# A decoder layer on one core: the first rstd moved to ScalarE, mask work moved into the attention loop, broadcast rows behind the weights, high weight parts on GpSimd, wider value matmuls

## The reference

```python
x = x + attention(layernorm(x), Wq, bq, Wk, bk, Wv, bv, Wo, bo)      # softmax(Q K^T / sqrt(16)), causal
n = layernorm(x)
x = x + softmax(where(mask, n @ ctx.T / 16, -1e30)) @ ctx            # zero where a batch has no valid token
n = layernorm(x)
logits = n @ router.T + rb;  score = softmax over the 4 largest logits
gate, up = (n @ gate_up[e] + bias)[..., ::2], [..., 1::2]            # all 16 experts e
x = x + sum_e score[e] * ((clip(up)+1) * min(gate,7) * sigmoid(1.702 gate) @ down[e] + dbias[e])
```

## Time and profile before

| | |
|---|---|
| time, median of 3 runs | 230.55 us (229.61 to 231.19) |
| profiled execution: its own time | 230.47 us |
| its span in the profile | 228.6 us |
| TensorE busy | 216.3 us, 95% |
| VectorE busy | 173.0 us, 76% |
| ScalarE busy | 127.8 us, 56% |
| GpSimd busy | 87.8 us, 38% |
| first matmul of the attention loop | us 16.54 |
| first matmul of the context scores | us 59.81 |

### The profile page before, as it was taken

How to read it: one execution, slowest core, us unless ns; L and a number is a source line. 1 busy time by engine, 2 the same in 40 slices (tenths; PEclk the granted TensorE clock), 3 DMA queues, 4 the chain that set the end, 5 groups by cost and what they waited for, 6 DMA issues and landing times.

```text
span 228.6 us, 4527 instructions
## 1 busy us (share of the span) xinstructions
PE 216.3 (95%) x1466; PEld 180.2 (79%) x1466; DVE 173.0 (76%) x434; ACT 127.8 (56%) x247; POOL 87.8 (38%) x67
## 2 busy tenths in 40 slices
PE   7899989998799799989999999999999999999995
PEld 2577857876478599768878988988988988998994
DVE  3489876779357755688798898898889789779655
ACT  2128999874343412835847657566476485395440
POOL 6622269941001100044254455447428428428000
PEclk9999999999799999999999999999999999999999
DMA  5993042000000000004214304404412322310002
GB/s 145 323 409 125 1 140 94 3 4 0 0 0 3 0 0 3 1 0 139 67 73 139 133 4 138 138 7 131 138 40 97 138 57 80 138 46 0 0 3 92
DMA packets 7998, 17.43 MB, mean 76 GB/s; under 512 B 928, under 2 KB 3120, under 8 KB 7856
## 3 DMA queue, kind: packets, MB, share of 16 engines
q1 hardware_dynamic: 7232, 16.52, 21.5%
q10 hardware_dynamic: 752, 0.73, 1.3%
HBM read 16.72 MB, written 0.52 MB: 75 GB/s over the span
## 4 chain that ended last, share of the span: by engine, by line
PE 74%; DVE 10%; ACT 6%; DMA 4%; issue 3%; ACTq 1%; DVEq 0%
PE PS L1121 35%; PE PS L1137 19%; DMA mask<-mask_d 4%; PE PS L1008 3%; PE PS L993 3%; ACT pr L418 3%; DVE masked L692 2%; PE PS L964 2%; PE PS L950 2%; PE PS L981 2%; PE PS L1166 2%; PE PS L1088 1%; DVE HL L813 1%; PE PS L936 1%; PE PS L1020 1%
## 5 line engine op out<-in xcount | busy, mean ns | idle before, releaser
L301 POOL TENSOR_TENSOR WLg<-raw_g,WHg 128x1024 fp32r<-128x1024 f32 x16 | 41.1, 2570 | 61.1 <-ACT WHg L388 61.1
L1121 PE MATMUL PS<-XH,WHg 128*128 128x512 f32 x120 | 47.0, 392 | 0.4 <-ACT pt L503 0.4
L1121 PE MATMUL PS<-XL,WHg 128*128 128x512 f32 x120 | 46.9, 390 | 0.0
L1121 PE MATMUL PS<-XH,WLg 128*128 128x512 f32 x120 | 46.7, 389 | 0.0
L813 DVE TENSOR_TENSOR HL<-pt,HH 128x512 fp32r<-128x512 f32 x30 | 30.8, 1026 | 12.2 <-ACT HH L512 12.2
L512 ACT ACTIVATE HH<-pt 128x512 fp32r<-128x512 f32 x30 | 18.9, 631 | 36.7 <-DVE pt L808 35.7
L808 DVE SCALAR_TENSOR_TENSOR pt<-pt 128x512 f32<-128x512 f32 x30 | 36.2, 1205 | 4.2 <-DVE pt L804 1.6
L1137 PE MATMUL PS<-WHd,HH 128*128 128x256 f32 x120 | 34.2, 285 | 0.9 <-DVE HL L813 0.8
L1137 PE MATMUL PS<-WLd,HH 128*128 128x256 f32 x120 | 34.0, 283 | 0.0
L1137 PE MATMUL PS<-WHd,HL 128*128 128x256 f32 x120 | 33.9, 283 | 0.0
L308 POOL TENSOR_TENSOR WLd<-raw_w,WHd 128x512 fp32r<-128x512 f32 x15 | 22.1, 1473 | 16.7 <-ACT WHd L394 16.7
(11 more groups left out here) (149 smaller groups left out, 357.9 us busy)
## 6 DMA issues: line engine op xcount, KB each, us to landing
raw_g<-we_d SPq DMA_DIRECT2D x16, 512.0 KB, 3.9
raw_w<-we_d SPq DMA_DIRECT2D x16, 256.0 KB, 2.7
ctxT<-ctxT_d SPq DMA_DIRECT2D x1, 1024.0 KB, 11.6
ctx_sb<-ctx_d SPq DMA_DIRECT2D x1, 1024.0 KB, 13.7
wqkv<-wqkv_d SPq DMA_DIRECT2D x3, 256.0 KB, 6.5
out_d<-x SPq DMA_DIRECT2D x4, 128.0 KB, 1.8
rows<-rows_d ACTq DMA_DIRECT2D x1, 264.0 KB, 6.3
x<-x_d ACTq DMA_DIRECT2D x2, 128.0 KB, 3.1
```

Source lines behind the costliest of these rows:

```text
L301: g.tensor_tensor(WLg[slot][:, :, :, :].rearrange("p k g f -> p (k g f)"), raw_g[slot][:, :], WHg[slot][:, :, :, :].rearrange("p k g f -> ...
L1121: i = t.matmul(PS[:, 2 * m + part, :], w[slot][:, k, part, m * P:(m + 1) * P], xx[:, k, :], start=(n == 0), stop=(n == 3 * KD - 1))
```

## The change

It has five parts.

1. **The first rstd.** ScalarE computes ln(variance + eps) and exp(-0.5 of it), two ACTIVATEs that wait for VectorE's last `bn_aggr`; GpSimd's power and VectorE's addition of eps fall away for this layernorm.
2. **The mask work.** `bup1` and `valid` leave VectorE's head. `bup1` now stands in step v = 7 and `valid`, with its wait for the mask, in step v = 8 of the loop.
3. **The transfers.** `rows` moves from ScalarE's queue to SyncE's, behind `wqkv`; the mask goes behind `wo`, and `dbias` behind the context, both on SyncE too.
4. **The high weight parts** of the first two experts are made by GpSimd, each right before its low part; ScalarE's three copies in the loop fall away.
5. **The value matmuls.** A unit had three groups of four matmuls with 128 columns; it now has four with 256 columns and four with 128.

```diff
             for j in (1, 0, 2):
                 sp.dma_start(wqkv[:, j], wqkv_d[:, j]).then_inc(qkv_in[j], 16)
+            sp.dma_start(rows[:, :], rows_d....to_broadcast([P, 2 * D + E])).then_inc(row_in, 16)
...
             sp.dma_start(wo[:, :, :], wo_d).then_inc(wo_in, 16)
+            sp.dma_start(mask8[:, :], mask_d....to_broadcast([P, B * M])).then_inc(mask_in, 16)
             sp.dma_start(ctxT[:, :, :], ctxT_d).then_inc(ctxT_in, 16)
...
+            sp.dma_start(dbias[:, :], dbias_d).then_inc(dbias_in, 16)
...
-            rstds(0)
...
+            def high_gate_up(e):
+                pool.wait_ge(raw_g_in[e], 16)
+                g.tensor_copy(WHg[e]..., raw_g[e][:, :]).then_inc(whg_done, 1)
...
+            act.wait_ge(eps_done, 1)
+            act.wait_ge(stat_done, 1)
+            a.activation(lnv[:, :], mv[:, :, 1], ACT.Ln, bias=eps[:, 0:1]).then_inc(ln_done, 1)
+            act.wait_ge(ln_done, 1)
+            a.activation(rstd[:, :], lnv[:, :], ACT.Exp, scale=-0.5).then_inc(rstd_done, 1)
...
-                if v == 3:
-                    high_gate_up(0, 0, 0)
...
-                if v == 4:
-                    high_down(0, 0, 0)
-                if v == 5:
-                    high_gate_up(1, 1, 0)
...
-            v_.tensor_scalar(bup1[:, :, :], gub[:, :, 1, :], 1.0, None, ALU.add)
-            dve.wait_ge(mask_in, 16)
-            v_.tensor_reduce(valid[:, :], mask8[:, :]...)
...
+                if v == TAIL - 4:
+                    v_.tensor_scalar(bup1[:, :, :], gub[:, :, 1, :], 1.0, None, ALU.add)
+                if v == TAIL - 3:
+                    dve.wait_ge(mask_in, 16)
+                    v_.tensor_reduce(valid[:, :], mask8[:, :]...)
...
-                for n, (qc, kc) in enumerate(((0, 0), (1, 0), (1, 1))):
-                    for h in range(HG):
-                        i = t.matmul(PS[HP * h:HP * (h + 1), 6, qc * P:(qc + 1) * P], vp[...],
-                                     pt[:, u % 2, h, n, :], start=(kc == 0), stop=(kc == qc))
+                for h in range(HG):
+                    t.matmul(PS[HP * h:HP * (h + 1), 6, 0:S], vp[:, b * QC, hg * HG + h, :],
+                             pt[:, u % 2, h, 0:QC, :]..., start=True, stop=False, ...)
+                for h in range(HG):
+                    i = t.matmul(PS[HP * h:HP * (h + 1), 6, P:S], vp[:, b * QC + 1, hg * HG + h, :],
+                                 pt[:, u % 2, h, QC, :], start=False, stop=True, ...)
```

More of the change, by code:

```diff
@@ L84, in decoder_layer @@
         half = sb("half", [P, NC])
+        eps = sb("eps", [P, 1])
+        lnv = sb("lnv", [P, NC])
         ones_f = sb("ones_f", [P, E])
@@ L171, in decoder_layer @@
         lnT_done = sem("lnT_done")
+        eps_done, ln_done = sem("eps_done"), sem("ln_done")
         xT_done = [sem(f"xT_done{b}") for b in range(B)]
@@ L233, in _ @@
                 sp.dma_start(wqkv[:, j], wqkv_d[:, j]).then_inc(qkv_in[j], 16)
+            sp.dma_start(rows[:, :], rows_d.rearrange("(a n) -> a n", a=1).to_broadcast([P, 2 * D + E])).then_inc(row_in, 16)
             for e in range(2):
@@ L264, in _ @@
             g.memset(half[:, :], -0.5)
+            g.memset(eps[:, :], EPS).then_inc(eps_done, 1)
             link(g.memset(ident[:, :], 0.0))
@@ L283, in rstds @@
             def rstds(n):
-                chunks = slice(0, NC) if n == 0 else slice((n - 1) % B * QC, (n - 1) % B * QC + QC)
+                chunks = slice((n - 1) % B * QC, (n - 1) % B * QC + QC)
                 pool.wait_ge(stat_done, n + 1)
                 g.tensor_tensor(rstd[:, chunks], ve[:, chunks], half[:, chunks], ALU.pow).then_inc(rstd_done, 1)
-            rstds(0)
             pool.wait_ge(row_in, 16)
@@ L554, in variances @@
             def variances(n, chunks):
-                dve.wait_ge(bn_done, NC if n == 0 else NC + n * QC)
+                dve.wait_ge(bn_done, NC + n * QC)
                 for c in chunks:
@@ L572, in _ @@
                 row_stats(x, c)
-            variances(0, range(NC))
+            dve.wait_ge(bn_done, NC)
+            for c in range(NC):
+                i = v_.bn_aggr(mv[:, c, :], stats[:, c, :])
+            i.then_inc(stat_done, 1)
             normalise(x, 0, range(NC))
@@ L600, in _ @@
             dve.wait_ge(param_in, 16)
-            v_.tensor_scalar(bup1[:, :, :], gub[:, :, 1, :], 1.0, None, ALU.add)
-            dve.wait_ge(mask_in, 16)
-            v_.tensor_reduce(valid[:, :], mask8[:, :].rearrange("p (b m) -> p b m", b=B), AX.X, ALU.max).then_inc(valid_done, 1)
             take_keys(0)
@@ L704, in _ @@
                     take_values(1)
+                if v == TAIL - 4:
+                    v_.tensor_scalar(bup1[:, :, :], gub[:, :, 1, :], 1.0, None, ALU.add)
+                if v == TAIL - 3:
+                    dve.wait_ge(mask_in, 16)
+                    v_.tensor_reduce(valid[:, :], mask8[:, :].rearrange("p (b m) -> p b m", b=B), AX.X, ALU.max).then_inc(valid_done, 1)
                 if v == TAIL + 4:
@@ L961, in values @@
                     pe.wait_ge(o_done, u)
-                for n, (qc, kc) in enumerate(((0, 0), (1, 0), (1, 1))):
-                    for h in range(HG):
-                        i = t.matmul(PS[HP * h:HP * (h + 1), 6, qc * P:(qc + 1) * P], vp[:, b * QC + kc, hg * HG + h, :],
-                                     pt[:, u % 2, h, n, :], start=(kc == 0), stop=(kc == qc))
+                for h in range(HG):
+                    t.matmul(PS[HP * h:HP * (h + 1), 6, 0:S], vp[:, b * QC, hg * HG + h, :],
+                             pt[:, u % 2, h, 0:QC, :].rearrange("p c q -> p (c q)"), start=True, stop=False, skip_group_check=True)
+                for h in range(HG):
+                    i = t.matmul(PS[HP * h:HP * (h + 1), 6, P:S], vp[:, b * QC + 1, hg * HG + h, :],
+                                 pt[:, u % 2, h, QC, :], start=False, stop=True, skip_group_check=True)
                 i.then_inc(av_done, 1)
```

11 lines of the change are left out of this document (8 added, 3 removed).

## The result

| | before | after |
|---|---|---|
| time, median of 20 runs each | 230.13 us (228.72 to 232.99) | 232.12 us (230.43 to 233.39) |
| ratio after / before, 95% interval | | 1.0068 [1.0040, 1.0096] |
| profiled execution: own time, span | 230.47, 228.6 us | 230.46, 228.7 us |
| granted TensorE clock, mean over the span | 0.993 | 1.000 |
| first scores | us 16.54 | us 15.16 |

The changed kernel is slower, by 0.7% in the ratio and 2.0 us in the medians. The forecast was 229.2, 1.3 us faster, and the time lies outside its range. The two profiled executions are equally long, and that hides two opposite amounts, in the last two rows: 3.3 us gained before expert 4, 3.4 lost behind it. Of the gain, 1.6 is no gain of the change. The profile of before has the stretch at half clock at us 60; this profile of after has none. Both levels occur in runs of either kernel.

What follows compares the result with a forecast made beforehand. TensorE was taken to bound the kernel from the first expert on, with gains only in the head and attention loop: 0.9 + 0.9 - 0.1 - 0.4 = 1.3 off 230.47 gives 229.2 us, own range 228.7 to 229.8 (wider: 227.5 to 230.5).

Steps and rivals of the forecast that it cites:

- From the first expert on the chain is TensorE alone: Experts: the change touches nothing there, so earlier gains reach the end as they are and no more can come.
- The first rstd: Head: two ACTIVATEs replace the power, 0.6 instead of 1.35, so normalisation starts at 6.12, 0.75 earlier.
- `rows`: Head: this transfer, now behind the value weights, lands at 10.7 (bounds 10.1 and 11.8), and then `xb` runs.
- a landing before 10: Head: the prediction called itself wrong if `rows` landed before 10 or after 12.
- The head: Before the first scores: 0.9 off of the 1.3 TensorE offers, scores at 15.6 instead of 16.54.
- The collision of the two low parts: Head: low queries, ready at 14.0, wait at the shared port for low keys until 14.8; without the lock 1.3 off.
- High weight parts: Attention loop: without ScalarE's copy of gate-up 1 the exponentials of v = 6 come earlier, 0.9 off.
- The second low queries: Attention loop, v = 2: VectorE can be held by GpSimd's subtraction, 0.1 on (0 to 0.5).
- `valid`: Attention loop: its 1.22 ahead of the masks of v = 9 mostly falls into slack, 0.4 on (0 to 1.22).
- The value matmuls: Attention loop: the new form streams as much, so nothing off, plus or minus 0.1 for each of 8 units.
- the 0.1 a unit: Attention loop, rival: four fewer matmuls take 0.1 off each of 8 units, 228.4 in all; chance 0.05.
- vanished dip: Half-clock stretch from 60.1 to 63.5, rival: a denser loop avoids it, 1.7 more off, 227.5; chance 0.09.

Runs made afterwards that it cites:

- the kernel with the mask beside it: The changed kernel with `bup1` and `valid` back in VectorE's head and the mask issued by ScalarE behind params; 231.98 us, ratio 1.0071 to the kernel before.
- part 2 undone: The changed kernel with `bup1` and `valid` back in VectorE's head and the mask issued by ScalarE; 231.98 us, ratio 1.0071 to the kernel before.
- part 4 undone: The changed kernel with ScalarE making the first experts' high weight parts again in the attention loop; 229.36 us, ratio 0.9964 to the kernel before.
- part 4 alone: The kernel before with only the first experts' high weight parts moved to GpSimd; 232.28 us, ratio 1.0116 to the kernel before.
- part 5 undone: The changed kernel with twelve value matmuls of 128 columns a unit again; 231.71 us, ratio 1.0079 to the kernel before.
- part 1 undone: The changed kernel with the first rstd by GpSimd's power and eps added on VectorE again; 231.73 us, ratio 1.0067 to the kernel before.
- the same wait: GpSimd's low gate-up part, two experts ahead, waits for VectorE's second product; kernel before 229.07 us, ratio 0.9923; changed kernel 228.12 us, ratio 0.9875.

## Why the prediction was wrong, point by point

**"From the first expert on the chain is TensorE alone, and nothing in the change touches that part, so a gain made earlier goes through to the end as it is": this is the step that failed.** TensorE alone was the chain only because every second step was free: half of the steps already had the product held for 2.90 in the kernel before, and in those the low part of the hidden values was done 0.6 ahead of its matmuls (135.44 against 136.07 in step 6), a margin that the next, free step restored. I had the rule of the port in hand for the head (2.26 beside 0.70) and that very row is from the experts' part, but I didn't ask how close the race was there. It was decided by 0.04 us. The change reached it by the number of GpSimd's instructions, 3 more ahead of the loop. Price: 118.4 - 115.0 = 3.4 us.

**The first rstd.** Forecast normalisation 6.12, measured 6.08. The two ACTIVATEs took 0.30 and 0.20 instead of 2 x 0.26. From the statistics to the normalisation it is 0.67 for a forecast of 0.6, and the statistics happened to end 0.11 earlier in this execution.

**`rows`.** The term was mis-sized. Forecast landing 10.7 with bounds 10.1 and 11.8; `xb` started at 9.41, outside them. The prediction named a landing before 10 as a sign that it was wrong. With less beside it the transfer sped up by more than I gave it (in the kernel with the mask beside it `xb` starts at 10.95). With `rows` back on ScalarE's queue `xb` starts no earlier (9.43), and the weights come later.

**The head.** Forecast 0.9 off, first scores at 15.6; measured 15.16, 1.38 off between the two profiles. The collision of the two low parts didn't happen (low keys 12.18 to 13.44, low queries at 14.13), because the landing was early. The collision itself is real: with part 2 undone `xb` starts at 10.95, the low keys run 13.69 to 14.98, and the low queries, started at 14.49, take 1.04 instead of 0.69. Heads with the same program differ from profile to profile: 15.83 to 16.62 in five kernels with the head of before (mean 16.26), 15.09 to 15.69 in six with that of after (mean 15.33). The difference of the means is 0.9, which is the forecast's number and not its mechanism: without a collision the forecast's own reasoning gives 1.3, so the agreement is luck. A single profile can't price a part of the head to a tenth.

**High weight parts.** Forecast 0.9 off. First scores to context scores: 42.90 in the kernel after, 43.79 with part 4 undone: 0.89. From the other side, 43.27 before and 42.44 with part 4 alone: 0.83. Right.

**The second low queries.** Forecast 0.1 on; nothing. They went first, and GpSimd's subtraction was held instead, 1.64 for a usual 1.3.

**`valid`.** Forecast 0.4 on. With part 2 undone the same stretch takes 42.37 instead of 42.90: 0.5. Right in the loop. But the wait for the mask that it should remove from the head was no longer there once the transfers had moved, so the part gains nothing to set against it.

**The value matmuls.** Forecast nothing; 0.79 a unit again, and with part 5 undone the stretch takes 42.94 against 42.90. Right; the 0.1 a unit that the prediction estimated from the matmuls' overhead didn't come.

**TensorE's clock.** The rival "vanished dip" got 0.09. In the profiled execution it vanished, in others not: before, part 1 undone and part 2 undone all show 0.993 and 35.7 us from context scores to the high gate-up part of expert 2, after shows 1.000 and 34.1. It is no property of the change. What had to be compared was runs at the same clock: at full clock the median span is 227.0 to 227.3 in the three groups of runs of before beside the experiments and 228.8 after, at a mean of 0.993 it is 228.5 to 228.6 and 230.5. At either, the changed kernel is 1.5 to 2.0 slower.

**Sum.** Head 0.9 and loop 0.4 off (43.27 to 42.90) are the 1.3 forecast. With the order fixed by the same wait in both, the kernels are at 229.07 and 228.12: the change by itself is then worth 1.0 us by the medians, of 10 and 4 runs whose ratios have overlapping intervals, so its size isn't shown well. Without the wait 3.4 come on top of the 1.3, which gives 2.1 slower, and the medians differ by 2.0. The sum of the terms came out, in the loop for its reasons and in the head by luck, and the term that was missing is larger than all of them.

## What to carry to other kernels

Where two engines want the same port within some hundredths of a microsecond, the order is part of the schedule: write it down with a wait, and choose who is first by whose result TensorE needs next. Before you say that a change doesn't touch a stretch, look in it for pairs that start within a tenth of each other in the trace, above all in a loop, since an order that repeats itself turns a lag of 0.09 into 0.3 for each expert. When a change costs or gains more than its parts explain, pad one engine's program with idle instructions as a control, before you look for a cause in the work.

## What the runs showed of the hardware that I had not expected

- Three one-column memsets on an idle GpSimd cost 2.1% [1.6, 2.6] in one kernel and gave 1.8% in the other (from 1.0068 to 0.9891): only the position of later instructions in GpSimd's program changes.
- One instruction in the loop, at a fixed number of the program in twelve kernels, starts 0.35 us late in the first pass and 0.09 in each later one; where it is a register instruction that runs ahead of a wait, nothing is late.
- Being held at the port cost less than waiting for the holder's semaphore: 8.64 against 8.80 us an expert.
- A ScalarE ACTIVATE of 4 columns took 0.20 to 0.30 us and GpSimd's power on them 1.02.
